# Layer 0's attention as one slot loop with column-tiled value products, and layer 1's output projection in two float32r weight parts

## The reference

```
q = relu(LN(x) @ W_fc + b_fc) @ W_q + b_q        (scaled by 16 ** -0.5)
k, v = relu(ctx @ W_fc + b_fc) @ W_k + b_k, the same @ W_v + b_v
out = softmax(q @ k.T) @ v                       256 x 512 scores for each of 64 pairs
x = x + tanh(g) * (relu(LN(x) @ W_fc + b_fc) + out)
```

```
y[b] += fp8(out[b, h] / smooth[h]) @ wproj[h]    h = 0..15, in each of two passes
```

## Time and profile before

| | us |
|---|---|
| median of 3 runs (lowest, highest) | 3851.64 (3850.96, 3852.68) |
| the profiled execution's own time | 3850.07 |
| its span in the trace | 3848.3 |
| mean granted TensorE clock of the span | 0.834 |
| PE busy in the span | 3190.8 (83%) |
| DVE busy | 2364.0 (61%) |
| ACT busy | 1691.9 (44%) |

### The profile page before, as it was taken

How to read it: one execution, slowest core, us unless ns; L and a number is a source line. 1 busy time by engine, 2 the same in 40 slices (tenths; PEclk the granted TensorE clock), 3 DMA queues, 4 the chain that set the end, 5 groups by cost and what they waited for, 6 DMA issues and landing times. The chain is left out here.

```text
span 3848.3 us, 52360 instructions
## 1 busy us (share of the span) xinstructions
PE 3190.8 (83%) x15855; PEld 1903.4 (49%) x15858; DVE 2364.0 (61%) x5551; ACT 1691.9 (44%) x3216; POOL 249.0 (6%) x245
## 2 busy tenths in 40 slices
PE   7889697777789889883699999924799899957899
PEld 4244464544555465451477777713311244435676
DVE  5832434777777677677444444467999866665432
ACT  4143121654555445441222222212699999923221
POOL 0000000311113101100000000031000000000000
PEclk9699798898899999995799999967755555578899
DMA  1000202000100000000200000001000000020000
GB/s 50 0 0 0 74 1 71 1 1 1 40 26 6 6 0 6 0 29 0 110 1 1 1 0 0 0 17 33 6 0 0 0 1 0 0 83 1 0 1 11
DMA packets 31307, 55.63 MB, mean 14 GB/s; under 512 B 3712, under 2 KB 23105, under 8 KB 28609
## 3 DMA queue, kind: packets, MB, share of 16 engines
q1 hardware_dynamic: 31168, 54.05, 4.1%
HBM read 52.99 MB, written 1.05 MB: 14 GB/s over the span
## 5 line engine op out<-in xcount | busy, mean ns | idle before, releaser
L917 ACT ACTIVATE a_probs<-psum,a_neg_max 128x512 f32<-128x512 f32 (+1 forms) x384 | 233.2, 612 | 355.2 <-DVE a_neg_max L910 313.8
L910 DVE TENSOR_REDUCE a_neg_max<-psum 128x2 f32<-128x1024 f32 (+1 forms) x192 | 200.9, 1047 | 284.1 <-PE psum L905 284.1
L905 PE MATMUL psum<-a_k_t,a_q_t 128*128 128x512 f32 (+1 forms) x768 | 325.4, 551 | 10.8 <-DVE a_k_t L1497 8.4
L962 PE MATMUL psum<-a_probs_t,a_vals 128*128 128x256 f32 x1280 | 309.5, 381 | 0.0
L1386 ACT ACTIVATE a_normed<-psum,a_head_bias,a_head_scale 128x128 f32<-128x128 f32 x448 | 168.2, 459 | 283.5 <-DVE a_head_bias L1488 282.2
L2221 ACT ACTIVATE a_v_all<-psum,a_ln 128x1024 f32<-128x1024 f32 x256 | 283.5, 1114 | 14.7 <-PE psum L2160 8.6
L2275 DVE TENSOR_REDUCE a_half_max<-psum 128x1024 f32 x256 | 289.6, 1197 | 0.0
L2138 PE MATMUL psum<-a_ks,a_qs 96*128 (+1 forms) x512 | 261.8, 615 | 29.1 <-ACT psum L2207 21.3
L2207 ACT ACTIVATE psum<-psum,a_half_max 128x1024 f32<-128x1024 f32 x256 | 278.6, 1088 | 3.3 <-DVE a_half_max L2275 3.3
L2160 PE MATMUL psum<-a_qs,a_ks 99*128 (+1 forms) x512 | 262.4, 616 | 5.5 <-ACT a_qs L2213 1.2
L2298 DVE TENSOR_SCALAR a_probs<-a_v_all 128x1024 bf16<-128x1024 f32 x256 | 177.7, 694 | 122.1 <-ACT a_v_all L2221 109.5
(11 more groups left out here) (447 smaller groups left out, 5834.9 us busy)
## 6 DMA issues: line engine op xcount, KB each, us to landing
a_ctx_t<-in_ctx_t_dram SPq DMA_DIRECT2D x12, 512.0 KB, 5.4
a_w_raw<-in_L_xattn_wproj_dram SPq DMA_DIRECT2D x2, 2048.0 KB, 18.5
f_w_silu<-in_L_ffn_gate_dram SPq DMA_DIRECT2D x1, 2112.0 KB, 11.2
f_w_mul<-in_L_ffn_up_dram SPq DMA_DIRECT2D x1, 2112.0 KB, 15.4
f_w_silu<-in_L_ffn_Wu_dram SPq DMA_DIRECT2D x1, 2048.0 KB, 8.9
f_w_mul<-in_L_ffn_Wg_dram SPq DMA_DIRECT2D x1, 2048.0 KB, 13.5
f_w_down<-in_L_ffn_Wd_dram SPq DMA_DIRECT2D x1, 2048.0 KB, 18.1
a_w_all<-in_L_xattn_wq_dram SPq DMA_DIRECT2D x1, 2048.0 KB, 8.9
```

What stands on the lines that cost most here:

```text
L905: mm = pe.matmul(core.bank(self.score_banks[r] + t)[:, 0:keys], q_t[:, t * P:(t + 1) * P], k_t, start=True, stop=True)
L910: v.tensor_reduce(self.neg_max[:, r, :], core.bank(self.score_banks[r], 2).rearrange("p (t n) -> p t n", t=TB)[:, :, 0:keys], AX.X, ALU.ma ...
L917: last = act.activation(self.probs[:, r, t, 0:keys], core.bank(self.score_banks[r] + t)[:, 0:keys], ACT.Exp, bias=self.neg_max[:, r, t:t + ...
L962: mm = pe.matmul(core.bank(4)[:, 0:S], vals[j], self.probs_t[:, r, j, :], start=(j == 0), stop=(j == n - 1))
```

## The change

Layer 0: the three stages become one loop of 76 slots, written out. The scores and maxima of pair `s` are done in slot `s`, its logits and exponential in slot `s + 7`. A ring of two banks (4 and 5) takes one score matmul each, and VectorE takes the maximum bank by bank, two instructions of 512 columns. After every fourth pair (one head) VectorE splits that head's 8 columns of maxima in four small instructions, TensorE turns them with one transpose, VectorE copies 24 rows out, and SP sends them with three DMAs from SBUF to the rows 96 to 98 of `qs`. `probs` has 8 slots, laid over `ctx_t`, `sup_t`, `xn_t` and `ref_t`. The products with the values are made once for a head's four batches: for each chunk of 128 keys four matmuls, whose outputs lie at partitions 0, 32, 64 and 96 of bank 6. ScalarE copies the bank, TensorE turns it with two 128 x 128 transposes, VectorE takes the reciprocals and the heads from there, and GpSimd divides and adds to `ref`, head by head. `ref + b_v` and a memset of bank 6 stand ahead of the loop.

Layer 1: `w_parts` and `cat` are `float32r`; two parts take the place of three bf16 ones; GpSimd's split has two instructions for four heads.

The diff, cut to its core:

```diff
-        ctx_t = sb("ctx_t", [P, 2, DK, C])
-        sup_t = sb("sup_t", [P, 2, DK, C])
+        SLOTS = 2 * B
+        probs = sb("probs", [P, SLOTS, CT * S])
+        ctx_t, sup_t = (probs[:, 2 * i:2 * i + 2, :].rearrange("p r (k n) -> p r k n", k=DK) for i in range(2))
+        xn_t, ref_t = (probs[:, 2 * i:2 * i + 2, :] for i in range(2, 4))
...
+        LAG = 7
+        SLOT_COUNT = LAG + STEPS + 5
+        RING, PRODUCTS, TURNS = 4, 6, 7
...
             @block.sync
+                for h in range(H):
+                    sp.wait_ge(rows_kept, h + 1)
+                    if h >= 2:
+                        sp.wait_ge(ROWS_IN[h % 2], 48 * (h // 2))
+                    for part in range(3):
+                        sp.dma_start(qs[KS + part:KS + part + 1, h * TOK:(h + 1) * TOK].rearrange("a (t n) -> a t n", t=NT),
+                                     max_rows[part * NT:(part + 1) * NT, h % 2, :]).then_inc(ROWS_IN[h % 2], 16)
...
             @block.gpsimd
+                for h in range(H):
+                    one = ref[:, :, h * DH:(h + 1) * DH]
+                    g.wait_ge(heads_kept, h + 1)
+                    g.tensor_tensor(heads[:, h, :, :], heads[:, h, :, :],
+                                    recip[:, h, :].unsqueeze(2).broadcast_to([P, NT, DH]), ALU.mult).then_inc(divided, 1)
+                    g.wait_ge(divided, h + 1)
+                    g.tensor_tensor(one, one, heads[:, h, :, :], ALU.add).then_inc(heads_done, 1)
...
             @block.tensor
-                attention_maxima_tensor(core, pe, qs, ks, C, scores_ready, max_ready)
-                pe.wait_ge(parts_ready, 1)
-                for h in range(H):
-                    out = act_unit(("row", h))
-                    transpose_maxima(core, pe, out, max_parts, h).then_inc(act_full, 1)
+                def scores(s):
+                    for q in range(TB):
+                        n = ring_use["scores", s, q]
+                        if n >= 2:
+                            pe.wait_ge(ring_free, n - 1)
+                        pe.matmul(ring(("scores", s, q)), qs[0:KS, s * S + q * P:s * S + (q + 1) * P],
+                                  ks[0:KS, s * C:(s + 1) * C], start=True, stop=True).then_inc(ring_full, 1)
...
+                def logits(i):
+                    if i % B == 0:
+                        h = i // B
+                        pe.wait_ge(ROWS_IN[h % 2], 48 * (h // 2 + 1))
+                    at_least(pe, probs_ready, i - 1)
...
+                def products(g, chunks):
+                    if chunks[0] == CT - 1:
+                        pe.wait_ge(probs_ready, (g + 1) * B)
+                        at_least(pe, heads_t_ready, g)
+                    for j in chunks:
+                        for b in range(B):
+                            mm = pe.matmul(core.bank(PRODUCTS)[32 * b:32 * b + W, 0:S], vals[:, g, b * CT + j, :],
+                                           probs[:, (g * B + b) % SLOTS, j * S:(j + 1) * S],
+                                           start=(j == CT - 1), stop=(j == 0), skip_group_check=True)
...
+                for s in range(SLOT_COUNT):
+                    if s < STEPS:
+                        scores(s)
+                    if rows_slot(s) is not None:
+                        rows(rows_slot(s))
+                    if 0 <= s - LAG < STEPS:
+                        logits(s - LAG)
+                    if group_at(s, B + 4) is not None:
+                        turn_heads(group_at(s, B + 4))
+                    for lag, chunks in ((B + 1, (3,)), (B + 2, (2,)), (B + 3, (1, 0))):
+                        if group_at(s, lag) is not None:
+                            products(group_at(s, lag), chunks)
...
             @block.scalar
+                for s in range(SLOT_COUNT):
+                    if 0 <= s - LAG < STEPS:
+                        exps(s - LAG)
+                    if group_at(s, B + 3) is not None:
+                        keep_products(group_at(s, B + 3))
...
             @block.vector
+                for s in range(SLOT_COUNT):
+                    if s < STEPS:
+                        maxima(s)
+                        if s % B == B - 1:
+                            split(s // B)
+                    if rows_slot(s) is not None:
+                        keep_rows(rows_slot(s))
+                    if group_at(s, B + 4) is not None:
+                        keep_heads(group_at(s, B + 4))
+                v.wait_ge(heads_done, H)
```

```diff
-        w_raw, w_parts = sb("w_raw", [P, H, D]), sb("w_parts", [P, 3, H, D], BF16)
+        w_raw, w_parts = sb("w_raw", [P, H, D]), sb("w_parts", [P, 2, H, D], F32R)
-        cat = sb("cat", [P, 4, S], BF16)
+        cat = sb("cat", [P, 4, S], F32R)
...
+                        g.tensor_copy(parts[:, 0], raw).then_inc(parts_step, 1)
+                        g.wait_ge(parts_step, split_steps(p, n) - 1)
+                        g.tensor_tensor(parts[:, 1], raw, parts[:, 0].bitcast(F32), ALU.subtract).then_inc(parts_step, 1)
...
-                                for part in range(3):
+                                for part in range(2):
                                     mm = pe.matmul(core.bank(7)[:, t * D:(t + 1) * D], cat[:, h % 4, t * P:(t + 1) * P], w_parts[:, part, h, :],
```

More of the change, by code:

```diff
@@ L8 @@
 FP8 = mybir.dt.float8e4
+F32R = mybir.dt.float32r
 ALU = mybir.AluOpType
@@ L385, in layer0_attention, with ring, rows_slot, group_at @@
         units += [("turn", TILES - 1, half) for half in range(2)]
-        before_rows = len(units)
-        units += [("row", h) for h in range(H)]
         count = {u: n + 1 for n, u in enumerate(units)}
         def act_bank(u): return core.bank(4 + (count[u] - 1) % 4)
[L390 to L394, removed]
+        LAG = 7
+        SLOT_COUNT = LAG + STEPS + 5
+        RING, PRODUCTS, TURNS = 4, 6, 7
+        ring_use = {}
+        for s in range(SLOT_COUNT):
+            if s < STEPS:
+                for q in range(TB):
+                    ring_use["scores", s, q] = len(ring_use)
+            if s >= 5 and (s - 5) % B == 0 and (s - 5) // B < H:
+                ring_use["rows", (s - 5) // B] = len(ring_use)
+        def ring(use):
+            return core.bank(RING + ring_use[use] % 2)
+        def rows_slot(s):
+            return (s - 5) // B if ("rows", (s - 5) // B) in ring_use and (s - 5) % B == 0 else None
+        def group_at(s, lag):
+            g, k = divmod(s - LAG - lag, B)
+            return g if k == 0 and 0 <= g < H else None
         with nc.Block() as block:
@@ L497, in logits @@
                     mm.then_inc(logits_ready, 1)
[L499 to L507, removed]
@@ L570, in _ @@
                         stack_key(v, stack[:, i % 2], rest, src).then_inc(stack_ready, 1)
[L571 to L586, removed]
+                v.tensor_tensor(ref[:, :, :], ref[:, :, :], rows[:, 3:4, :].broadcast_to([P, NT, D]), ALU.add).then_inc(rest_ready, 1)
@@ new lines, in _, with maxima @@
+                v.wait_ge(act_free, len(units))
+                v.memset(core.bank(PRODUCTS)[:, 0:S], 0.0).then_inc(products_zero, 1)
+                def maxima(s):
+                    h, b = divmod(s, B)
+                    for q in range(TB):
+                        v.wait_ge(ring_full, ring_use["scores", s, q] + 1)
+                        v.tensor_reduce(neg_max[:, h, b * TB + q:b * TB + q + 1], ring(("scores", s, q)),
+                                        AX.X, ALU.max, negate=True).then_inc(ring_free, 1)
@@ new lines, in split @@
+                def split(h):
+                    parts, rest, src = max_parts[:, h, :, :], max_rest[:, h, :], neg_max[:, h, :]
+                    v.drain()
+                    v.tensor_copy(parts[:, 0, :], src)
+                    v.drain()
+                    v.tensor_tensor(rest, src, parts[:, 0, :], ALU.subtract)
+                    v.drain()
+                    v.tensor_copy(parts[:, 1, :], rest)
+                    v.drain()
+                    v.tensor_tensor(parts[:, 2, :], rest, parts[:, 1, :], ALU.subtract).then_inc(parts_ready, 1)
```

94 lines of the change are left out of this document (58 added, 36 removed).

## The result

The changed kernel takes 3715.77 us (median of 4 runs, 3710.49 to 3718.73) against 3851.3; the ratio is 0.9646 (95% interval 0.9629 to 0.9663). The forecast was 3725. The profiled execution's span is 3713.8 us, 134.5 less. The first step of the next stage begins at 277.1 in place of 396.7, so 119.6 us come from layer 0. The other 15 are in layer 1's attention, which lasts 1069.8 us in place of 1084.9.

A forecast was written before the change was run, and what follows sets the result against it. Layer 0's attention was taken to pay for its engines one after the other, and TensorE to bound layer 1's pass 1. 3850.1 - 113 - 13.5 = 3723.6 profiled, the median 1.6 above: 3725 us, range 3698 to 3785.

The forecast's parts named there:

- The bound before: Layer 0's attention before the change: a different engine full in each stage, paid one after the other, 268.2 us.
- The products: Layer 0's slot loop: 16 product calls a head overlap by half across four column tiles, 3.65 us of 7.30.
- case B: Rival, layer 0's products: four tiles side by side, VectorE the bound, 7.6 us a head with coupling; 3712 us, 18%.
- The price of one instruction: Layer 0's products: 0.228 us for each instruction of a 32-bit call, two instructions a call.
- case D: Rival, layer 0's loop: TensorE stops at each change between whole array and tiles, 1.1 us a head; 3742 us, 9%.
- VectorE: Layer 0's slot loop: VectorE works 7.2 us a head, 5.52 of it maxima at 0.69 each.
- The coupling: Layer 0's ring: next score matmul stands behind logits and products, chain 1.8 us a slot; 8.3 taken for four.
- A: The forecast's own case: layer 0's products overlap by half, TensorE 7.4 us a head; 3725 us, 42%.
- The DMA wait: Layer 0's loop: a head's first logits wait for three DMAs, 3.3 us; charged 0.3 a head, 5 in all.
- Start, tail, clock: Layer 0's loop outside full slots: maxima alone 10.9 us, half clock 2, slots without scores 9.8, last head 8.6.
- float32r: Layer 1's projection: 0.108 us a call, 0.43 a head for 0.65; 13.8 us saved in pass 1, 0 in pass 0.
- Cases E and F: Rivals, layer 1's projection: float32r at half the bf16 rate, 3754 us, 5%; as slow as 32 bits, 3857 us, 4%.

## Why the prediction was right, and where it was not

The direction and the size were as forecast: 113 + 13.5 us against about 120 + 15. The time came 9 us under it. Inside both terms errors met, and one part of the second came from a place that the prediction had ruled out. Step by step:

*The bound before.* Engines paid for one after the other: confirmed, since even in the version without overlap of tiles, with TensorE at 95%, layer 0 ends 48 us earlier than before.

*The products*, half of 7.30: this step failed, and it is the largest. The four tiles run fully side by side, 1.73 us a head, case B's price. The reasoning from program order was wrong: the exchanged order costs nothing, so what waits for a busy tile does not hold back the others. The 2.38x that the Trainium skill has for three tiles (TensorE: Matmul & The Clock Gate, Part 3: Packing small matmuls) would have given 3.1 us, an estimate from that page; here two tiles give 2.0x and four 4.0x in streaming time, and the run decides. (The mean per slot was also taken as 0.97, where 3.65 / 4 is 0.91; that changes little.)

*The price of one instruction*: 0.228 was read off eight in 1.82 us. It is 0.216 and one change of 0.1, which the row of before held all along. So case D was true in kind and a little over half as dear as I had it: 0.1 a change, 0.6 a head, in place of 1.1. The rule of the Trainium skill that a change of tiling mode drains TensorE (TensorEngine Tiling (Array Packing), Key Properties) fits this, 0.1 us each; that a drain is what costs it is not shown.

*VectorE.* A maximum of 512 columns was priced by its duration, 0.69; back to back they start 0.60 apart, 4.8 a head in place of 5.5. The small ones were near: 0.17 each, the split 0.9, rows 0.20, heads 0.36. Its own work is thus 6.3 us a head in place of 7.2.

*The coupling.* Named rightly (the next score behind logits and products), and two tiles at 9.32 confirm it, but undersized. A head lasts 8.05 us and VectorE's own work is 6.3, so 1.8 is lost to the coupling (its waits for score matmuls say the same). The prediction laid 0.9 over the fullest engine in A and 0.4 in B, whose condition, four tiles side by side, is the one that came true: B said 7.6 a head. The products too dear by 1.9 us and VectorE too dear by 0.9 hid this and left 8.05 against 8.3. The right time was partly luck.

*The DMA wait.* 3.1 us from the first issue to the logits (236.97 to 240.05 by the timeline), as estimated (3.3), though an issue took 0.635 on SP in place of 0.42. It was charged 5 us. In the changed kernel the logits start only 0.16 us late (0.60 behind the score matmul in place of 0.44), and TensorE waits for VectorE soon after (0.48 us at 235.04, one head earlier), so it costs about nothing; this is read from the timeline, no run shows it alone. With three banks it is 0.76 us late, and on the path.

*Start, tail, clock.* The loop ran from 127.65 to 274.08, 146.4 us, where 150 (155 with the DMA waits) was forecast. The lower clock of the first slots came as said, but lasted to about 158. Slots 7 to 14 took 158.93 - 139.15 = 19.8 us, where eight steady slots take 16.1 and four of these had no products yet; 2 us were charged. After the loop the next stage starts 3.0 us later in place of 2.2.

*float32r.* One instruction a call, 0.12 in place of 0.108; 0.18 us a head in place of 0.216. The count failed more than the price: the prediction took 64 heads, and the four batches of pass 1 give 6.5 us in place of 13.8, because only ten turns of each batch have all four blocks. Cases E and F were wrong. The steady heads of pass 0 hide it, as forecast. That nobody waits for GpSimd's split was wrong: VectorE did, and TensorE behind it, and 5.6 us of pass 0 came back with the shorter split. So the 13.5 against 15 is near by luck as well.

## What to carry to other kernels

Price an instruction by the distance between starts in a long run of its kind, and put what is left at the ends down to the change of kind; durations of single instructions made VectorE's maxima too dear by 15%, and an average over eight hid a cost that is paid per change. When stages are merged into one loop, count the banks between two engines: with two, each waits for the other at every uneven slot although neither is full, and a third was worth more than the order of issue; and look at what was hidden in the old slack (here a DMA chain of 3.1 us) before the slack is removed. Count the turns in which an engine really has all its blocks before multiplying a saving by the number of heads. And an engine that is idle 94% of the time can still hold up another one: look at what runs beside it.

## What the runs showed of the hardware

Four 32-bit matmul calls with 17 output partitions at partitions 0, 32, 64 and 96 run in the time of one: 8 instructions stream in 1.73, 0.86 and 0.43 us with one, two and four tiles, and 16 in 0.99 and 1.01 us, change included, in two orders with four tiles. A change between 128-column matmuls and such tiles costs about 0.1 us, with one, two and four tiles alike. A float32r call of 256 columns is one instruction and 0.12 us, against 0.108 for bf16 and 0.43 for 32 bits. The granted clock held 1.00 through a loop in which TensorE was busy 87%, having been 0.50 in the slots before the products joined in at 151.6 and for 6 us more. Beside a GpSimd instruction of 2.1 us that reads two tiles, VectorE instructions of 0.29 and 0.43 us lasted 2.20 and 2.26, in both kernels that have the old split. Maxima of 512 columns from PSUM last 0.69 us each and start 0.60 apart.
